# Turned rows kept in memory, and a pair's full-precision work in one stretch, in a kernel of two MoE layers around a state-space layer

## The chip, the cores and the metric

The kernel runs on one core of a Trainium2 chip. The metric is the device time of one execution in microseconds (us), taken as the median of several runs. Another execution was recorded by the hardware profiler; its rows are the source of all durations below. Engines are called PE (TensorE), ACT (ScalarE), DVE (VectorE), POOL (GpSimd) and SP (SyncE, which issues most DMAs here).

## The reference, cut to what matters

4096 tokens (2 x 2048) of 512 values pass through three parts: a feed-forward (FFN) layer, a state-space layer (Mamba-2), and the same FFN layer again with the same weights; each is added to its input. The change lies in the FFN:

```python
h = layernorm(x)                                  # eps 1e-5, no weights
logits = h @ router_w.T                           # 64 experts
topk_idx = top_k(logits + bias, 4); topk_w = softmax scores of these, summing to 1
out  = sum over experts e: scatter(topk_w * (silu(h_e @ gate_w[e].T) * (h_e @ up_w[e].T)) @ down_w[e].T)
out += (silu(h @ sh_gate.T) * (h @ sh_up.T)) @ sh_down.T   # shared expert, 1024 wide
x = x + 0.5 * out
```

Each expert has 64 slots (CAP) for tokens and an inner width of 128.

## The kernel before, in words

`ffn` builds one FFN; it is called twice, with the tags a and b (`prior` is set for b), and `mamba` stands between. All three are pieces of one program on each engine, and the order on each engine is written out by hand: an engine runs its instructions strictly in order, and semaphores join them.

**Blocks and units.** The shared expert goes through 16 blocks of 256 tokens (NS, BS). A block has 4 units (UN), each of which computes 256 of the 1024 inner columns: `gate_or_up` for the gate (24 matmuls of 256 columns), the same for up, and `down` of the unit before (12 matmuls of 512 columns). These run in a faster fp32 format (fp32r) with every operand split into a high and a low part, `three` matmuls for one product. Between the three parts stand positions g = 3u, 3u+1, 3u+2, where other work is put in.

**Turning the rows for the shared expert.** The matmuls need the normalised tokens turned, with the 512 features on the partitions: `hts_hi[b % 2]` and `hts_lo[b % 2]`. For each block ACT's `normed` makes `hs` from the rows `xs` (two passes, L580 and L585), PE's `turn_s` (L724) turns it in two halves of 4 transposes, into the PSUM bank `p_ts`, ACT's `turned_s` (L590) copies the high part and DVE's (L1009) the rest. For block b+1 this is done in units 1 to 3 of block b.

**Routing.** In blocks 0 to 7 the router works on 512 tokens (r = b, that is blocks 2r and 2r+1): DVE's `norm_apply` writes the normalised rows `hr`, PE's `turn_r` turns slice k (of 4) into `p_x0` (L766), ACT's and DVE's `turned_r` copy it into `htr_hi[k % 2]` and `htr_lo[k % 2]` (L609, L951), and `logits_turned` multiplies (L778). Slices 0 and 1 come in unit 0, slices 2 and 3 in unit 1; on ACT slice 2 comes ahead of `product_hi` of unit 1. So the same rows are turned twice, once here and once in `turn_s`. POOL sends the rows to their experts' slots in memory (L459), and clears (L468, L499).

**Pairs.** The 64 experts are taken as 32 pairs, from unit 39 on, two pairs in each unit. For pair q: SP loads rows and weights (`load_pair`, three buffers), PE turns the rows (`turn_rows`, L803), multiplies (`expert_gate_up`, L814, into columns 0 to 255 of `p_x1`), turns the product (`turn_prod`, L821, into further columns of `p_x1`) and does `expert_down` (L829); all that is in full fp32. `begins`, `turns_rows` and `turns_product` say at which position what is done; the turned product stands in the middle of a gate or behind up. ACT copies the result into one of 5 buffers `y` (L636), and POOL adds it to the output in memory (`add_pair`, L479), each addition waiting for the one before; blocks 10 to 13 are added in the same chain (`add_block`, L475). At the end of FFN b POOL's `merge` (L485) adds the second half of the output to the first in memory.

**SP.** One list for each block: the load of the next 512 tokens `xr` (L420), the store of the finished block before (L423), then, over the positions, pairs and the rows `xs` of the block after next (`load_xs`, L350).

Of the kernel before, what the change touches and what calls it, by code (L numbers as in the profile page):

```python
# [13 lines left out]
P = 128  # L14
# [168 lines left out]
def ffn(nc, tag, c, sems, src, acc, xg, shw, routw, routb, ew, first_token, clear_slots, merge_all, prior=None):  # L183
# [13 lines left out]
    with ExitStack() as ctx:  # L197
# [70 lines left out]
        xs_loaded, x_stored = [sem(f"xs_loaded{u}") for u in range(XB)], sem("x_stored")  # L268
        hs_mid, hs_ready, ts_full = sem("hs_mid"), sem("hs_ready"), sem("ts_full")
# [27 lines left out]
        turned_in = lambda b, half: p_gate if b == 0 and half == 1 else p_ts  # L297
# [12 lines left out]
        def turns_rows(g):  # L310

            u, p = divmod(g, 3)
            q = 2 * (u - PAIR_UNIT) + p
            return q if p > 0 and 0 <= q < PAIRS else None

        def turns_product(g):


            u, p = divmod(g, 3)
            q = 2 * (u - PAIR_UNIT) + (0 if p == 1 else -1)  # L320
            return q if p < 2 and 0 <= q < PAIRS else None
# [20 lines left out]
        def sync(sp):  # L342
# [9 lines left out]
            def load_pair(q):  # L352
# [12 lines left out]
                sp.dma_start(w[u][:], ew[q]).then_inc(w_loaded[u], 16)  # L365

# [34 lines left out]
            def program():  # L401
# [42 lines left out]
        def gpsimd(pool):  # L444
# [46 lines left out]
            def program():  # L491
# [43 lines left out]
                pool.wait_ge(hs_mid, NS * TS)  # L535
# [22 lines left out]
        def scalar(act):  # L558
# [10 lines left out]
            def normed(b):  # L569
                rows_of = xs[:, b % XB, :, :]  # L570
                if b == 0 and not prior:
                    rows_of = xr
                else:
                    act.wait_ge(xs_loaded[b % XB], 16 * (b // XB + 1))
                act.wait_ge(mean_ready, norms(b * TS))
                act.wait_ge(rstd_ready, norms(b * TS))
                wait(act, ts_full, 2 * b)
                for j in range(TS):
                    at = b * TS + j
                    a.activation(hs[:, j, :], rows_of[:, j, :], ACT.Identity,  # L580
                                 bias=neg_mean[:, at:at + 1]).then_inc(hs_mid, 1)
                for j in range(TS):
                    at = b * TS + j
                    act.wait_ge(hs_mid, at + 1)
                    a.activation(hs[:, j, :], hs[:, j, :], ACT.Identity,  # L585
                                 scale=rstd[:, at:at + 1]).then_inc(hs_ready, 1)

            def turned_s(b, half):
                act.wait_ge(ts_full, 2 * b + half + 1)
                a.activation(hts_hi[b % 2][:, 2 * half:2 * half + 2, :], turned_in(b, half)[:, :, :], ACT.Copy).then_inc(hts_hi_ready, 1)  # L590
# [47 lines left out]
            def experts_at(g):  # L638
                q = begins(g)
                if q is not None and q < PAIRS:  # L640
                    expert_silu(q)
                if q:
                    expert_out(q - 1)
                q = turns_rows(g)
                if q is not None:
                    rows_out(q)

            def early(step):
                if step == 0:

                    act.wait_ge(prior.x_stored[2], 16 * len(range(2, NM, XM)))
                    normed(0)
                if step == 1:
                    split(0)
                    turned_s(0, 0)
                    turned_s(0, 1)
# [4 lines left out]
            def program():  # L661
                if not prior:
                    split(0)
                    normed(0)
                    turned_s(0, 0)
                    turned_s(0, 1)
# [5 lines left out]
                for b in range(NS):  # L672
                    for u in range(UN):
                        i, g = b * UN + u, b * POS + 3 * u
                        routes, more = b < NR, b + 1 < NS
# [9 lines left out]
                        if more and u == 2:  # L685
                            turned_s(b + 1, 0)
                        if more and u == 3:
                            turned_s(b + 1, 1)
# [9 lines left out]
                        if more and u == 1:  # L698
                            normed(b + 1)
# [9 lines left out]
        def tensor(pe):  # L709
# [7 lines left out]
            def turn_s(b, half):  # L717
                pe.wait_ge(hs_ready, (b + 1) * TS)
                if b > 0:
                    pe.wait_ge(hts_ready, 2 * b + half)  # L720
                for kk in range(2):
                    k = 2 * half + kk
                    for j in range(TS):
                        mm = t.matmul(turned_in(b, half)[:, kk, j * P:(j + 1) * P], hs[:, j, k * P:(k + 1) * P], c.ident[:],  # L724
# [3 lines left out]
            def gate_or_up(i, g, out, full, free):  # L728
                b, u = divmod(i, UN)
                if g == 0 and u == 0:  # L730
                    pe.wait_ge(hts_ready, 2 * b + 2)
# [75 lines left out]
            def expert_gate_up(q):  # L807
# [3 lines left out]
                wait(pe, pt_ready, q)  # L811
# [20 lines left out]
            def experts_at(g):  # L832
                q = begins(g)
                if q is not None and q < PAIRS:
# [1356 lines left out]
```

## Time and profile before

| what | value |
|---|---|
| median of 3 runs | 2375.12 us (2374.7 to 2375.79) |
| the profiled execution | 2374.74 us, of which the recorded span is 2373.0 us |
| PE busy | 2328.0 us (98%), 16700 matmuls |
| DVE, ACT, POOL busy | 59%, 40%, 29% |
| FFN a, state space, FFN b | about 0 to 720, 720 to 1640, 1620 to 2373 us |
| granted TensorE clock | 0.994 over the span |
| DMA | mean 123 GB/s; 254 to 289 GB/s in the stretches with pairs |

The span is what the profiler recorded; the execution's own time is 1.7 us more. The busy time of PE sums durations that overlap, so the share says that PE hardly rests, not what one matmul costs; for that the starts in the timeline are read. FFN b begins while the state-space part ends, since the parts overlap by some instructions.

### The profile page before, as it was taken

To read this page: it belongs to the slowest core of one execution; us is meant where nothing else is said; L and a number is where in the kernel's file an instruction comes from. 1 tells how busy PE (TensorE), PEld (TensorE's weight loads), DVE (VectorE), ACT (ScalarE), POOL (GpSimd) and SP (SyncE) were. 2 spreads that over 40 slices of the span, in tenths; PEclk is the share of its full clock that TensorE was granted. 3 is DMA by queue.
4 is the path that set the end of the run, shared out by engine and by line. 5 is a ranking of instruction groups with operands and counts; after the bars stand their busy time and mean duration, and the time that the engine had idled before them with its cause. 6 is when DMAs were issued, how large, how long until landed. Compare 5 with 4: busy or idle time off the path is not lost.

```text
span 2373.0 us, 41894 instructions
## 1 busy us (share of the span) xinstructions
PE 2328.0 (98%) x16700; PEld 2059.6 (87%) x16700; DVE 1393.6 (59%) x3240; ACT 950.3 (40%) x1650; POOL 680.9 (29%) x526
## 2 busy tenths in 40 slices
PE   6999999999999999999999999999999999999997
PEld 6999999777788899998998898998999999877787
DVE  6777762223228777777777777778777763222221
ACT  5333322333327455554545555455433232323331
POOL 1244443111220323232322222321144444112121
PEclk9999999999999999999999999999999999999999
DMA  8644213899844111111111111104263411799958
GB/s 265 205 144 153 86 64 126 261 279 282 253 93 133 36 36 28 28 28 28 27 28 27 28 27 28 28 19 161 74 222 109 141 65 37 254 289 287 276 106 176
DMA packets 102785, 292.81 MB, mean 123 GB/s; under 512 B 22530, under 2 KB 22786, under 8 KB 91904
## 3 DMA queue, kind: packets, MB, share of 16 engines
q1 hardware_dynamic: 55248, 198.87, 23.3%
q0 software_dynamic: 47344, 91.27, 17.3%
q8 instruction: 133, 2.18, 0.4%
q14 instruction: 60, 0.49, 0.1%
HBM read 197.28 MB, written 151.80 MB: 147 GB/s over the span
## 4 chain that ended last, share of the span: by engine, by line
PE 96%; DVE 2%; ACT 1%; issue 1%; DMA 0%; DVEq 0%; POOL 0%; SPq 0%; ACTq 0%
PE m_p_ab L1614 5%; PE m_p_ab L1615 5%; PE m_p_ab L1616 5%; PE m_p_x L1616 3%; PE m_p_x L1615 3%; PE m_p_x L1614 3%; PE p_up_b L713 3%; PE p_up_a L713 3%; PE p_gate_a L713 3%; PE p_up_b L715 3%; PE p_up_b L714 3%; PE p_gate_b L713 3%; PE p_gate_a L715 3%; PE p_gate_a L714 3%; PE p_up_a L715 3%; PE p_up_a L714 3%
## 5 line engine op out<-in xcount | busy, mean ns | idle before, releaser
L1927 DVE SCALAR_TENSOR_TENSOR m_xt<-m_ssm,m_convw,m_xt 128x256 f32<-128x256 f32 x384 | 219.1, 584 | 58.1 <-ACT m_ssm L1483 48.9
L459 POOL DMA_INDIRECT slot_rows<-a_hr,a_slot_now x128 | 130.4, 1019 | 152.1 <-PE p_gate_a L715 96.5
L459 POOL DMA_INDIRECT slot_rows<-b_hr,b_slot_now x128 | 130.3, 1018 | 151.8 <-PE p_gate_b L715 96.5
L1614 PE MATMUL m_p_ab<-m_ht_hi,m_wi_b_hi 128*128 128x256 f32 x576 | 163.6, 284 | 3.3 <-ACT m_gate L1455 3.3
L1615 PE MATMUL m_p_ab<-m_ht_lo,m_wi_b_hi 128*128 128x256 f32 x576 | 161.7, 281 | 0.0
L1616 PE MATMUL m_p_ab<-m_ht_hi,m_wi_b_lo 128*128 128x256 f32 x576 | 161.7, 281 | 0.0
L713 PE MATMUL p_gate_a<-a_hts_hi,a_w_hi 128*128 128x256 f32 x512 | 149.4, 292 | 1.7 <-DVE a_hts_lo L1009 1.4
L713 PE MATMUL p_up_a<-a_hts_hi,a_w_hi 128*128 128x256 f32 x512 | 147.9, 289 | 0.0
L713 PE MATMUL p_gate_b<-b_hts_hi,b_w_hi 128*128 128x256 f32 x512 | 147.4, 288 | 0.3
L713 PE MATMUL p_up_b<-b_hts_hi,b_w_hi 128*128 128x256 f32 x512 | 147.7, 288 | 0.0
L1389 POOL TENSOR_TENSOR m_state_dec<-m_state,m_etot 128x1024 f32<-128x1024 f32 x31 | 74.0, 2387 | 255.4 <-ACT m_etot L1499 255.4
L715 PE MATMUL p_gate_a<-a_hts_hi,a_w_lo 128*128 128x256 f32 x512 | 146.3, 286 | 0.0
L714 PE MATMUL p_gate_a<-a_hts_lo,a_w_hi 128*128 128x256 f32 x512 | 146.2, 285 | 0.0
L715 PE MATMUL p_up_a<-a_hts_hi,a_w_lo 128*128 128x256 f32 x512 | 144.8, 283 | 0.0
L715 PE MATMUL p_up_b<-b_hts_hi,b_w_lo 128*128 128x256 f32 x512 | 144.7, 283 | 0.0
L714 PE MATMUL p_up_a<-a_hts_lo,a_w_hi 128*128 128x256 f32 x512 | 144.6, 282 | 0.0
L715 PE MATMUL p_gate_b<-b_hts_hi,b_w_lo 128*128 128x256 f32 x512 | 144.4, 282 | 0.0
L714 PE MATMUL p_up_b<-b_hts_lo,b_w_hi 128*128 128x256 f32 x512 | 144.4, 282 | 0.0
L714 PE MATMUL p_gate_b<-b_hts_lo,b_w_hi 128*128 128x256 f32 x512 | 144.3, 282 | 0.0
L1015 DVE TENSOR_TENSOR b_prod<-b_silu,p_up_b 128x512 f32<-128x512 f32 x64 | 44.0, 687 | 165.0 <-PE p_up_b L715 164.5
L1015 DVE TENSOR_TENSOR a_prod<-a_silu,p_up_a 128x512 f32<-128x512 f32 x64 | 44.0, 687 | 149.0 <-PE p_up_a L715 148.1
L1481 ACT ACTIVATE m_xt<-m_p_ab,m_convb,m_convw 128x256 f32<-128x256 f32 x128 | 72.2, 564 | 143.4 <-PE m_p_ab L1616 143.4
(374 smaller groups left out, 7518.8 us busy)
## 6 DMA issues: line engine op xcount, KB each, us to landing
a_ew<-in_ew SPq DMA_DIRECT2D x32, 1536.0 KB, 7.6
b_ew<-in_ew SPq DMA_DIRECT2D x32, 1536.0 KB, 7.3
after_ffn<-a_zeros POOLq DMA_DIRECT2D x6, 2048.0 KB, 9.2
out<-b_zeros POOLq DMA_DIRECT2D x6, 2048.0 KB, 9.2
slot_rows<-a_zeros POOLq DMA_DIRECT2D x1, 8336.0 KB, 40.0
a_rows<-slot_rows SPq DMA_DIRECT2D x32, 260.5 KB, 8.0
b_rows<-slot_rows SPq DMA_DIRECT2D x32, 260.5 KB, 8.1
a_xs<-in_x SPq DMA_DIRECT2D x16, 512.0 KB, 4.2
```

Source lines behind the costliest of these rows:

```text
L459: g_.indirect_dma_start(out=xg, out_offset=bass.IndirectOffsetOnAxis(ap=slot_now[r % HR][:, at:at + 1], axis=0), in_=hr[r % HR][:, j, :], ...
L713: t.matmul(out, l_hi, r_hi_, start=first, stop=False)
L714: t.matmul(out, l_hi, r_lo_, start=False, stop=False)
L715: return t.matmul(out, l_lo, r_hi_, start=False, stop=last)
L1015: v.tensor_tensor(prod[:, i % 2, :, :], silu[:, i % 2, :, :], p_up[:, :, :], ALU.mult).then_inc(prod_ready, 1)
L1389: g.tensor_tensor(state_dec[:], state[:], etot[:, j, :].unsqueeze(2).to_broadcast([P, NH, HP]), ALU.mult).then_inc(state_dec_ready, 1)
L1481: a.activation(xt[:, m, :], ab_of(J_SSM[m])[:, 0:BM], ACT.Identity, bias=convb[:, m:m + 1], scale=convw[:, m, HALO:CONV]).then_inc(tap_rea ...
L1614: t.matmul(out, l_hi, r_hi_, start=first, stop=False)
L1615: t.matmul(out, l_hi, r_lo_, start=False, stop=False)
L1616: return t.matmul(out, l_lo, r_hi_, start=False, stop=last)
L1927: ins_ = v.scalar_tensor_tensor(xt[:, m, :], ssm[:, m, i:i + BM], convw[:, m, i:i + 1], xt[:, m, :], ALU.mult, ALU.add)
```

## The change

1. The high and low turned parts of the router's pass are stored to a new tensor in memory, `turned`, [16 blocks, 128, 2, 1024], by `store_turned`: for each slice k two stores of 256 KB with runs of 1 KB. `load_turned` brings them back for blocks 1 to 15, two loads of 512 KB with 4 KB per partition. `normed`, `turn_s` and `turned_s` remain for block 0 alone.
2. ACT's copy of slice k into `htr_hi` now also waits until the stores of slice k-2 have landed (`turned_stored`), and the first gate of blocks 1 to 15 waits for `hts_loaded`.
3. For each pair PE now does at one position: the turned product of the pair before, gate/up of this pair, the rows of the next, down of the pair before. `turns_rows` and `turns_product` are gone; the turned product goes to the bank `p_ts`, which is free there now.
4. `finish` waits for `xs_loaded` itself, and the two waits elsewhere that counted `hs_mid` and `ts_full` are rewritten.

The diff, cut to its core:

```diff
+        turned_stored, hts_loaded = [sem(f"turned_stored{u}") for u in range(2)], sem("hts_loaded")
...
+        FIRST_ROWS = 3 * PAIR_UNIT - 1
...
+            def store_turned(r, k):
+
+                for i, (part, ready) in enumerate(((htr_hi, htr_hi_ready), (htr_lo, htr_ready))):
+                    sp.wait_ge(ready, r * KD + k + 1)
+                    sp.dma_start(turned[2 * r:2 * r + 2, :, i, k * BS:(k + 1) * BS].rearrange("b p t -> p b t"),
+                                 part[:, k % 2, :].bitcast(F32).rearrange("p (b t) -> p b t", b=2)).then_inc(turned_stored[k % 2], 16)
+
+            def load_turned(b):
+                for v in range(2):
+                    sp.wait_ge(turned_stored[v], 32 * (KD // 2) * (b // 2 + 1))
+                if b >= 2:
+                    sp.wait_ge(up_full, (b - 1) * UN)
+                for i, part in enumerate((hts_hi, hts_lo)):
+                    sp.dma_start(part[b % 2][:, :, :].bitcast(F32).rearrange("p k t -> p (k t)"),
+                                 turned[b, :, i, :]).then_inc(hts_loaded, 16)
...
+                    if b < NR:
+                        store_turned(b, 0)
                     if 1 <= b <= NR + 1:
                         sp.wait_ge(acc_ready, b * TS)
                         sp.dma_start(acc_s[b - 1], xs[:, (b - 1) % XB, :, :]).then_inc(x_stored, 16)
+                    if b < NR:
+                        for k in range(1, KD):
+                            store_turned(b, k)
+                    if b + 1 < NS:
+                        load_turned(b + 1)
...
-                pool.wait_ge(hs_mid, NS * TS)
+                pool.wait_ge(xs_loaded[(NS - 1) % XB], 16 * ((NS - 1) // XB + 1))
...
                 if f >= 2:
                     act.wait_ge(lt_done, f - 1)
+                    act.wait_ge(turned_stored[k % 2], 32 * (f // 2))
                 a.activation(htr_hi[:, k % 2, :], p_x0[:], ACT.Copy).then_inc(htr_hi_ready, 1)
...
+                if g == 0 and u == 0 and b > 0:
+                    pe.wait_ge(hts_loaded, 32 * b)
...
-                    if g == 0 and m == 1 and turns_product(3 * i) is not None:
-                        turn_prod(turns_product(3 * i))
...
-                t.matmul(p_x1[:, 2 * F:2 * F + P], eprod[:, q % 2, :], c.ident[:],
+                t.matmul(p_ts[:, 0, 0:P], eprod[:, q % 2, :], c.ident[:],
...
             def experts_at(g):
                 q = begins(g)
+                if g == FIRST_ROWS:
+                    turn_rows(0)
+                if q:
+                    turn_prod(q - 1)
                 if q is not None and q < PAIRS:
                     expert_gate_up(q)
+                if q is not None and q + 1 < PAIRS:
+                    turn_rows(q + 1)
                 if q:
                     expert_down(q - 1)
-                q = turns_product(g)
-                if q is not None and g % 3:
-                    turn_prod(q)
-                q = turns_rows(g)
-                if q is not None:
-                    turn_rows(q)
...
-                        if more and u == 3:
-                            turn_s(b + 1, 1)
```

How the instructions move, at two places. First PE, a unit with pairs in FFN a. Before, behind up stand the turned product (of `a_eprod`) and rows of a pair, and behind `down` the gate/up (`a_ew`, `a_xt`), down (`a_pt`) and rows of others (two pieces):

```order
L715 MATMUL p_up_a<-a_hts_hi_55,a_w_lo 128x256
L821 MATMUL p_x_a<-ident,a_eprod 128x128
L803 MATMUL p_x_a<-ident,a_rows_96 128x128 x4
L713 MATMUL p_out_a<-a_w_hi,a_act_hi 128x512
L714 MATMUL p_out_a<-a_w_lo,a_act_hi 128x512
```

```order
L715 MATMUL p_out_a<-a_w_hi,a_act_lo 128x512
L814 MATMUL p_x_a<-a_ew_99,a_xt 64x256 x8
L829 MATMUL p_x_a<-a_ew_98,a_pt 64x512 x2
L803 MATMUL p_x_a<-ident,a_rows_94 128x128 x4
L713 MATMUL p_gate_a<-a_hts_hi_55,a_w_hi 128x256
L714 MATMUL p_gate_a<-a_hts_lo_56,a_w_hi 128x256
```

With the change the four kinds stand together, here behind `down`; nothing stands behind up, and the line numbers are the changed file's:

```order
L724 MATMUL p_out_a<-a_w_hi,a_act_lo 128x512
L827 MATMUL p_ts_a<-ident,a_eprod 128x128
L820 MATMUL p_x_a<-a_ew_99,a_xt 64x256 x8
L810 MATMUL p_x_a<-ident,a_rows_94 128x128 x4
L835 MATMUL p_x_a<-a_ew_98,a_pt 64x512 x2
L722 MATMUL p_gate_a<-a_hts_hi_55,a_w_hi 128x256
L723 MATMUL p_gate_a<-a_hts_lo_56,a_w_hi 128x256
```

The turned product now goes ahead of a gate/up, and rows stand between gate/up and down.

Second, SP at the start of FFN a (`a_hr_71`, `a_xs` and `a_hr_72` are also the staging places of the weights). Before, behind the last piece of weights:

```order
L350 DMA a_xs<-in_x 128x2x512
L420 DMA a_xr<-in_x 128x4x512
L350 DMA a_xs<-in_x 128x2x512
L420 DMA a_xr<-in_x 128x4x512
L423 DMA after_ffn<-a_xs 128x2x512
L350 DMA a_xs<-in_x 128x2x512
```

With the change, from the load of `xr` for routing block 1 on to the load of `xs` for block 2:

```order
L428 DMA a_xr<-in_x 128x4x512
L363 DMA turned_rows<-a_htr_hi 128x2x256
L363 DMA turned_rows<-a_htr_lo 128x2x256
L363 DMA turned_rows<-a_htr_hi 128x2x256
L363 DMA turned_rows<-a_htr_lo 128x2x256
L363 DMA turned_rows<-a_htr_hi 128x2x256
L363 DMA turned_rows<-a_htr_lo 128x2x256
L363 DMA turned_rows<-a_htr_hi 128x2x256
L363 DMA turned_rows<-a_htr_lo 128x2x256
L372 DMA a_hts_hi_55<-turned_rows 128x1024
L372 DMA a_hts_lo_56<-turned_rows 128x1024
L342 DMA a_xs<-in_x 128x2x512
```

All eight stores and the two loads of block 1 stand ahead of the load of `xs`, and each store waits for its copy.

## Rows read from the trace of the kernel before

**Rows 1.** The page: chain of waits by engine, and the SP queue's bytes and share.
```profile
q1 hardware_dynamic: 55248, 198.87, 23.3%
...
PE 96%; DVE 2%; ACT 1%; issue 1%; DMA 0%; DVEq 0%; POOL 0%; SPq 0%; ACTq 0%
```

**Rows 2.** Groups of PE by line and form: xcount, busy us, mean ns, idle before.
```profile
L724 PE MATMUL p_ts_a<-ident,a_hs 128*128 128x128 f32 x124 | 19.0, 277 | 11.7 <-ACT a_hs L585 11.7
```

**Rows 3.** PE's timeline around one turning group: start us, us, engine, line, what.
```profile
290.78 0.60 PE L724 MATMUL p_ts_a<-ident,a_hs 128*128 128x128 f32 x4
291.13 0.48 PE L713 MATMUL p_out_a<-a_w_hi,a_act_hi 128*128 128x512 f32 x1
291.45 0.39 PE L714 MATMUL p_out_a<-a_w_lo,a_act_hi 128*128 128x512 f32 x1
291.68 0.39 PE L715 MATMUL p_out_a<-a_w_hi,a_act_lo 128*128 128x512 f32 x1
```

**Rows 4.** PE's timeline, turned rows of pairs in FFN a and what follows.
```profile
507.54 0.60 PE L803 MATMUL p_x_a<-ident,a_rows 128*128 128x128 f32 x4
507.89 0.48 PE L713 MATMUL p_out_a<-a_w_hi,a_act_hi 128*128 128x512 f32 x1
...
513.61 0.66 PE L803 MATMUL p_x_a<-ident,a_rows 128*128 128x128 f32 x4
514.02 0.37 PE L713 MATMUL p_gate_a<-a_hts_hi,a_w_hi 128*128 128x256 f32 x1
```

**Rows 5.** Block 0 of FFN b: timelines of SP, ACT, PE; median us to landing.
```profile
1656.78 0.51 SPq L350 DMA_DIRECT2D b_xs<-after_mamba  x1
...
b_xs<-after_mamba SPq DMA_DIRECT2D x1, 512.0 KB, 7.9
...
1657.86 0.60 ACT L609 ACTIVATE b_htr_hi<-p_x_b 128x512 fp32r<-128x512 f32 x1 [0.20 <-PE p_x_b L766]
...
1661.00 0.60 PE L766 MATMUL p_x_b<-ident,b_hr 128*128 128x128 f32 x4
```

**Rows 6.** Block 0 of FFN a: timelines of SP and ACT; us to landing.
```profile
32.06 0.51 SPq L350 DMA_DIRECT2D a_xs<-in_x  x1
...
a_xs<-in_x SPq DMA_DIRECT2D x1, 512.0 KB, 6.9
...
36.24 0.60 ACT L609 ACTIVATE a_htr_hi<-p_x_a 128x512 fp32r<-128x512 f32 x1
```

**Rows 7.** Block 2 of FFN a: SP's store of a block, its landing, and PE.
```profile
113.52 0.37 SPq L423 DMA_DIRECT2D after_ffn<-a_xs  x1
...
after_ffn<-a_xs SPq DMA_DIRECT2D x1, 512.0 KB, 5.8
...
119.57 0.60 PE L766 MATMUL p_x_a<-ident,a_hr 128*128 128x128 f32 x4
```

**Rows 8.** POOL's timeline in FFN b, additions of pairs (in brackets: idle before, releaser).
```profile
2211.66 1.63 POOL L479 DMA_INDIRECT out<-b_y,b_row_no  x1 [11.88 <-DMA out<-b_xs]
...
2261.70 1.56 POOL L479 DMA_INDIRECT out<-b_y,b_row_no  x1 [4.38 <-ACT b_y L636]
...
2276.47 1.63 POOL L479 DMA_INDIRECT out<-b_y,b_row_no  x1 [5.69 <-DMA out<-b_xs]
...
2305.87 1.55 POOL L479 DMA_INDIRECT out<-b_y,b_row_no  x1 [4.38 <-issue]
```

**Rows 9.** Windows (busy us of PE, PEld, DVE, ACT, POOL; PEclk, DMA share, GB/s); end.
```profile
2100.00:2200.00 100.00, 100.00 (x713) 75.52 (x712) 30.22 (x124) 30.10 (x60) 20.07 (x13) 1.00 0.90 273
2290.00:2300.00 10.00, 10.00 (x74) 9.46 (x73) 2.67 (x4) 1.83 (x3) 1.78 (x3) 1.00 0.42 52
2325.00:2360.00 35.00, 35.00 (x236) 32.03 (x235) 6.81 (x10) 4.91 (x8) 3.54 (x4) 1.00 1.04 212
...
q0 software_dynamic: 460, 2.43, 103.1%
...
2359.67 0.39 PE L715 MATMUL p_out_b<-b_w_hi,b_act_lo 128*128 128x512 f32 x1
```

More of the change, by code:

```diff
@@ L295, in ffn @@
                  hr[2][:, :, :].rearrange("p j d -> p (j d)")[:, 0:PIECE]]
-        turned_in = lambda b, half: p_gate if b == 0 and half == 1 else p_ts
+        turned_in = p_ts, p_gate
         norms = lambda at: at // TS + 1 if at < TR else at // TR + 2
@@ L567, in split, with normed, turned_s @@
                 a.activation(w_hi[:, i * PIECE:(i + 1) * PIECE], stage[slot_of[o]], ACT.Copy).then_inc(w_hi_done, 1)
-            def normed(b):
-                rows_of = xs[:, b % XB, :, :]
-                if b == 0 and not prior:
-                    rows_of = xr
[L573 to L577, printed above, removed]
+            def normed():
+                rows_of = xs[:, 0, :, :]
+                if prior:
+                    act.wait_ge(xs_loaded[0], 16)
+                else:
+                    rows_of = xr
+                act.wait_ge(mean_ready, 1)
+                act.wait_ge(rstd_ready, 1)
                 for j in range(TS):
-                    at = b * TS + j
                     a.activation(hs[:, j, :], rows_of[:, j, :], ACT.Identity,
-                                 bias=neg_mean[:, at:at + 1]).then_inc(hs_mid, 1)
+                                 bias=neg_mean[:, j:j + 1]).then_inc(hs_mid, 1)
                 for j in range(TS):
-                    at = b * TS + j
-                    act.wait_ge(hs_mid, at + 1)
+                    act.wait_ge(hs_mid, j + 1)
                     a.activation(hs[:, j, :], hs[:, j, :], ACT.Identity,
[L586 to L590, printed above, removed]
+                                 scale=rstd[:, j:j + 1]).then_inc(hs_ready, 1)
+            def turned_s(half):
+                act.wait_ge(ts_full, half + 1)
+                a.activation(hts_hi[0][:, 2 * half:2 * half + 2, :], turned_in[half][:, :, :], ACT.Copy).then_inc(hts_hi_ready, 1)
             def gate_silu(i):
@@ L674, in program @@
                         i, g = b * UN + u, b * POS + 3 * u
-                        routes, more = b < NR, b + 1 < NS
+                        routes = b < NR
                         gate_silu(i)
@@ L715, in three, with turn_s @@
                 return t.matmul(out, l_lo, r_hi_, start=False, stop=last)
[L717 to L720, printed above, removed]
+            def turn_s(half):
+                pe.wait_ge(hs_ready, TS)
                 for kk in range(2):
@@ L723, in turn_s @@
                     for j in range(TS):
-                        mm = t.matmul(turned_in(b, half)[:, kk, j * P:(j + 1) * P], hs[:, j, k * P:(k + 1) * P], c.ident[:],
+                        mm = t.matmul(turned_in[half][:, kk, j * P:(j + 1) * P], hs[:, j, k * P:(k + 1) * P], c.ident[:],
                                       is_transpose=True, start=True, stop=True)
@@ L862, in program @@
                         i, g = b * UN + u, b * POS + 3 * u
-                        routes, more = b < NR, b + 1 < NS
+                        routes = b < NR
                         if i > 0 or not prior:
@@ L880, in program @@
                             logits_turned(b, 2)
-                        if more and u == 2:
-                            turn_s(b + 1, 0)
                         if routes and u == 3:
@@ L1024, in finish @@
                 dve.wait_ge(down_done, (b + 1) * UN)
-                if b == 0 and not prior:
-                    dve.wait_ge(xs_loaded[0], 16)
+                dve.wait_ge(xs_loaded[b % XB], 16 * (b // XB + 1))
                 if b == NS - 1:
@@ L1098, in program @@
                         i, g = b * UN + u, b * POS + 3 * u
[L1099 removed]
+                        routes = b < NR
                         if routes and u == 0 and b > 0:
@@ L2104, in build @@
         with Phase(nc) as s:
-            first = ffn(nc, "a", c, s, ins["x"], after_ffn, xg, *weights, 0, True, False)
+            first = ffn(nc, "a", c, s, ins["x"], after_ffn, xg, turned, *weights, 0, True, False)
             state_space = first.follow = mamba(nc, c, s, after_ffn, after_mamba, ins, first)
```

83 lines of the change are left out of this document (32 added, 51 removed).

## The prediction

> **What bounds the kernel now.** I read the chain of waits first, because it says which engine's time is the kernel's time: 96% of it is TensorE (PE) [rows 1]. PE is therefore worth a second look at every edit, and DVE and ACT only where somebody waits for them. Then I read PE's groups by line for what is removed [rows 2], PE's timeline for what such a piece takes of the engine, which is less than its duration [rows 3, 4], the block that starts each FFN for the new waits [rows 5, 6], a routing block in a busy stretch [rows 7], and last the queue of the GpSimd (POOL) and the DMA load at the end [rows 8, 9]. That last look matters most: from 2325 to 2360 us the DMA engines are busy all the time [rows 9], with the software queue's merges alone, and PE's last matmul starts at 2359.67. The end is thus held by two things at once, and only one of them gets shorter by PE's savings.
>
> The sum is made against the profiled execution, 2374.7 us (span 2373.0); the median of the runs is 2375.1. I count 0.2%, 4.8 us, as what a measurement can tell from no change.
>
> **Removed: the turning of the shared expert's rows.** Blocks 1 to 15 of each FFN lose two groups of four turnings each, 60 groups and 240 matmuls in all. One turning lasts 277 ns [rows 2], but they overlap: from the group's start at 290.78 to the next matmul at 291.13 are 0.35 us, and the matmul behind takes 0.32 us to its successor where the next takes 0.23 [rows 3]. So a group costs 0.35 + 0.09 = 0.44 us of PE. 30 groups x 0.44 = 13.2 us in each FFN. The Trainium skill (TensorE: Matmul & The Clock Gate, Part 4: PE-mode transpose) gives about 275 ns for one 128x128 transpose in a kernel. The trace agrees for the duration, and by that figure as a cost the 240 would be worth 66 us; the spacing in the timeline decides against it. ACT loses four scalings and two copies for each block, DVE two subtractions; neither is on the chain there, so I count nothing.
>
> **Moved: the pairs' work.** Per unit of two expert pairs PE had four excursions into full precision (product in the middle of a gate, pair work after gate, product and rows after up, pair work after down) and now has two. Leaving one costs about 0.09 us, as above, so two fewer give 0.2 us. Against it, rows turned directly behind full-precision work take 0.41 us instead of 0.35 [rows 4], once more per unit. How a turned product sits ahead of a pair's first matmul no row shows: between 0 and 0.1 us each. That leaves 0 to 0.3 us per unit, 0 to 5 us for 16 units; I take 2. The product's copy on DVE is now hidden by the gate/up and rows matmuls of the same stretch, where DVE is idle but for the two adds that close a block.
>
> **Added: the store, and who waits for it.** For each routing block SP issues 8 stores of 256 KB, and for each block from 1 on two loads of 512 KB. The copy of the k-th slice (ACT) now waits until the store of slice k-2 has landed. Behind that copy stand DVE's low half, PE's next turning and, on ACT, a weight split and the hi half of the product. In steady blocks the store of slice 0 goes out behind the 1 MB load of the next rows, so it lands about where the store of 512 KB lands now: in the busiest block issued at 113.52 and 5.8 us under way, so at 119.3, just when PE wants to turn slice 3, at 119.57 [rows 7]; the copy takes 0.6 us [rows 5] and the low half about as much again. I take 1.5 us for FFN a and 0.5 for b, between nothing and 1.5 per block.
>
> Block 0 is worse. In FFN b SP comes to its loop only after a 1 MB piece; today the load issued at 1656.78 takes 7.9 us, to 1664.7 [rows 5]. The store of slice 0 takes its place. The copy of slice 2, at 1657.86 today, moves to about 1664.5, the low half is ready at 1666, and PE, which today turns slice 3 at 1661.00, waits 4.5 us; the last slice adds about 1, and the clock may fall after the idle time, so 6 us. In FFN a the same place is taken by a load issued at 32.06 that lands 6.9 us later, at 39.0, against a copy at 36.24 [rows 6]: 2 us. A store is twice as many and half as large packets as that load, so both could be longer. The loads of turned rows for block 1 are needed only about two units after the last store, and later ones have two units of slack; I count nothing. If that cover goes, PE waits at the first gate of a block.
>
> FFN a: -13.2 - 2 + 2 + 1.5 = -11.7 us.
>
> **The end of FFN b.** From the second pair on, POOL's additions form a chain in which each waits for the one before [rows 8]. It runs far behind PE: the last addition starts at 2305.87, while PE's last pair is in unit 55 of 64. It is followed by a block, by reads and by the merges that fill the engines to the end. What PE gains after the chain has begun it cannot pass on. Before that point FFN b has 20 of its 30 groups: -8.8 us, + 6 + 0.5 of waits, so -2.3 us. During the chain four blocks load 1 MB each. At 23.3% of the span for 198.87 MB [rows 1] one such load takes 2.9 us of all engines, in 62 us a share of 0.05. An addition takes 50.04/7 = 7.15 us at a share of 0.90 and 29.4/5 = 5.9 at 0.42 [rows 8, 9], 2.6 us per unit of share, so 0.13 x 30 = 4 us later. The bounds are 0, and 12 us if each load simply stands ahead of the chain. In FFN a the same lag first shows in ACT's wait for a free y buffer; from there to PE there is about one pair's distance, 7 us, which I take as enough. With that cover gone PE would wait for `y_ready`.
>
> Sum: -11.7 - 2.3 + 4 = -10.0 us, so 2364.7, against 2374.7. PE itself would end 20 us earlier and then wait for nobody.
>
> **Rivals.**
> (1) PE sets the end after all: the merges start as much earlier as PE does. Then FFN b gives -13.2 - 2 + 6.5 = -8.7 and the time is 2374.7 - 20.4 = 2354.3. The full DMA engines speak against it [rows 9]. Chance 0.09.
> (2) The stores land fast: each store is half of the transfers in [rows 5 to 7], and packets of two queues may share better than I think. Then the waits of 2 + 1.5 + 6 + 0.5 go, and the time is 2354.7. Chance 0.11. The Trainium skill (DMA: Bandwidth & Descriptors, Anatomy of one DMA) gives 2.0 us plus bytes/436 GB/s, an estimate of 2.6 us for 256 KB, and this case would be its result; the rows of loaded queues (5.8 to 7.9 us) are above it.
> (3) A turning costs its duration: 60 groups at 0.60 us. FFN a then gains 18 instead of 13.2 and b 12 instead of 8.8 before its chain: 2356.7. Chance 0.02.
> (4) The chain of additions is hit harder: 12 us in b and some 4 us of PE waiting for y in a. 2364.7 + 8 + 4 = 2376.7. The share of 0.90 speaks for it. Chance 0.17.
> (5) Slower: the stores' small packets share the engines with the software queue's large ones, and the copy of slice 2 or 3 is late in every routing block, not in block 0 alone. At 2 us for 13 of them, less the 2 counted, it is +24: 2388.7. It turns into a loss from about 0.9 us per block. The block of [rows 7] is at the edge; the others' traffic is lighter. Chance 0.15.
>
> **How the numbers follow.** My case has 0.46, its own range 2356 to 2373. With rivals 1 to 3, faster by over 0.2% (under 2370.4) comes to 0.67, a few of my own case lying above; within 0.2% is rival 4 and that rest, 0.18; slower is rival 5, 0.15. The range takes in rival 1 and rival 4: 2353 to 2378.
>
> **What would show it.** PE's rows on the turning of hs fall from 248 matmuls to 16. The copy L609 (its line will move) shows waits for a DMA in block 0: some 6 us in b, 3 in a, and under 1 elsewhere; PE shows one idle time of 4 to 5 us at slice 3 of b. FFN b's first addition comes 13 to 15 us earlier, the last one some 10, and the DMA engines are full until the end while PE stops 8 us or more ahead of them. I am wrong if PE's end still sets the span, if the copy waits in steady blocks, or if the first gate of a block waits for its load.

## The result, and the profile after

The changed kernel takes 2403.95 us (median of 4 runs, 2403.28 to 2410.25) against 2375.36 beside it (2374.7 to 2375.79): a ratio of 1.0111, 95% interval 1.0088 to 1.0135. It is 28.6 us slower; the predicted gain was 10. The profiled spans differ by the same amount, 2401.6 against 2373.0, so the traces can carry the explanation. At the first silu of FFN b 18.3 us of the loss have come up, the other 10.3 come in FFN b.

First the page of the changed kernel: TensorE's busy time, the SP queue, the chain of waits by engine, and two groups of PE (busy us, mean ns).

```profile
PE 2326.4 (97%) x16460; PEld 2033.5 (85%) x16460; DVE 1360.8 (57%) x3180; ACT 854.9 (36%) x1470; POOL 677.4 (28%) x526
q1 hardware_dynamic: 98704, 263.90, 31.3%
PE 92%; DMA 4%; DVE 2%; ACT 1%; issue 1%; SPq 0%; POOL 0%; DVEq 0%; ACTq 0%
...
L731 PE MATMUL p_ts_a<-ident,a_hs 128*128 128x128 f32 x4 | 1.1, 427 | 11.5 <-ACT a_hs L598 11.5
L835 PE MATMUL p_x_a<-a_ew,a_pt 128*64 128x512 f32 x128 | 34.5, 617 | 0.4 <-DVE a_pt L1054 0.4
```

The turnings are gone (4 of 124 are left in p_ts_a, [rows 2]), 240 matmuls in all, but PE's busy time is only 1.6 us below the 2328.0 of before. The SP queue moves 65 MB more than in [rows 1], in 43456 more packets, and DMA has 4% of a chain that had none. Next, who waits (us in total, times, longest), for PE and for ACT.

```profile
PE p_x_a L773 <- DVE a_htr_lo L953: 10.0, 4, 5.4
PE p_x_b L773 <- DVE b_htr_lo L953: 9.6, 5, 6.6
PE p_gate_a L722 <- DMA a_hts_lo<-turned_rows: 8.5, 1, 8.5
PE p_x_a L785 <- DVE a_htr_lo L953: 5.7, 1, 5.7
...
ACT a_htr_hi L623 <- DMA turned_rows<-a_htr_lo: 19.0, 5, 8.7
ACT b_htr_hi L623 <- DMA turned_rows<-b_htr_lo: 13.9, 4, 8.6
```

These are large waits but few: ACT's copy of a slice waits 9 times in 64. PE's first two sums hold one wait each that is not new: 5.4 us before the turning at 28.89, where the kernel before waits 4.9, and 2.0 at 1671.65, the same as before. To find where the time goes I laid the two traces side by side, by the start of ACT's 64 silus in each FFN; a step in the distance is a place of gain or loss.

| place | change against before |
|---|---|
| FFN a, block 0 from second to third unit | +12.4 us |
| FFN a, first unit of block 1 | +10.4 |
| FFN b, block 0 from second to third unit | +8.5 |
| each removed group of turnings | -0.43 |
| blocks 2 and 3 of both FFNs (a: 1.4; b: 0.7 and 0.5) | +2.6 in all |
| each unit that works on two pairs | +0.65 |
| end: from PE's last matmul to the end of the span | +4.3 |

With 60 groups (-25.8) and 15 such units in each FFN (+19.5) these come to 31.9. The first unit of block 0 in FFN a gives 1.7 back and the stretch between the FFNs 1.0; 0.6 are left over.

The first place, in SP's timeline of FFN a's block 0 (start, us, line, what):

```profile
31.46 0.40 SPq L428 DMA_DIRECT2D a_xr<-in_x  x1
31.90 0.51 SPq L363 DMA_DIRECT2D turned_rows<-a_htr_hi  x1
...
41.51 1.00 SPq L363 DMA_DIRECT2D turned_rows<-a_htr_lo  x1
52.03 0.36 SPq L363 DMA_DIRECT2D turned_rows<-a_htr_hi  x1
52.76 0.36 SPq L363 DMA_DIRECT2D turned_rows<-a_htr_lo  x1
70.68 0.33 SPq L372 DMA_DIRECT2D a_hts_hi<-turned_rows  x1
```

and ACT's and PE's timelines (in brackets the idle time before, and what ended it), with the windows of 10 us (busy us of PE, PEld, DVE, ACT, POOL; then granted clock, DMA share, GB/s):

```profile
40.16 0.60 ACT L623 ACTIVATE a_htr_hi<-p_x_a 128x512 fp32r<-128x512 f32 x1 [5.28 <-DMA turned_rows<-a_htr_lo]
51.41 0.60 ACT L623 ACTIVATE a_htr_hi<-p_x_a 128x512 fp32r<-128x512 f32 x1 [8.68 <-DMA turned_rows<-a_htr_lo]
...
81.90 0.58 PE L722 MATMUL p_gate_a<-a_hts_hi,a_w_hi 128*128 128x256 f32 x1 [8.54 <-DMA a_hts_lo<-turned_rows]
...
50.00:60.00 10.00, 7.21 (x47) 7.02 (x48) 5.60 (x18) 1.79 (x3) 1.03 (x1) 0.71 1.03 282
70.00:80.00 10.00, 3.36 (x27) 2.47 (x25) 6.91 (x14) 0.64 (x1) 0.00 (x0) 0.82 1.06 234
80.00:90.00 10.00, 8.10 (x50) 8.10 (x51) 0.00 (x0) 0.60 (x1) 0.00 (x0) 0.67 0.40 155
```

Three things stand in these rows. The DMA engines are full (1.03, 1.06): POOL's clearing of the slots, 8336 KB, runs from about 34 to 80 us. Of the 256 KB stores the one of 41.51 takes 19.4 us to land and that of 52.76 takes 17.9; the load for block 1 can't be issued before, and lands 10.8 us later. And behind the idle times TensorE's granted clock is below full (0.71, 0.67), which makes each wait dearer than its own length. Behind the wait of 8.5 us the gate's matmuls first follow each other after 0.21 us instead of 0.12, and the delay is 10.4 us. In block 0 PE idles 1.2, 2.2 and 5.7 us, 9.1 in all, and the delay is 12.4.

### The profile page after: what moved, and what is told of

It is laid out like the page before. It is cut to its first block, busy times and chain, and to the rows that moved or that the text cites. A ratio compares the mean times of both kernels' runs of the same rounds, so it can differ in the third digit from the quotient of the medians.

```text
span 2401.6 us, 41242 instructions
## 1 busy us (share of the span) xinstructions
PE 2326.4 (97%) x16460; PEld 2033.5 (85%) x16460; DVE 1360.8 (57%) x3180; ACT 854.9 (36%) x1470; POOL 677.4 (28%) x526
## 4 chain that ended last, share of the span: by engine, by line
PE 92%; DMA 4%; DVE 2%; ACT 1%; issue 1%; SPq 0%; POOL 0%; DVEq 0%; ACTq 0%
PE m_p_ab L1610 5%; PE m_p_ab L1611 4%; PE m_p_ab L1612 4%; PE m_p_x L1612 3%; PE m_p_x L1611 3%; PE m_p_x L1610 3%; PE p_up_b L722 3%; PE p_gate_b L722 3%; PE p_gate_a L722 3%; PE p_x_a L820 3%; PE p_x_b L820 3%; PE p_up_a L722 2%; PE p_out_b L722 2%; PE p_up_b L724 2%; PE p_up_b L723 2%; PE p_out_b L724 2%
```

## The experiments

Each ran beside the kernel before. In these runs the kernel before spread over 2372 to 2392 us, so each time is read by its ratio, and the mechanism by the distance of the silus to those of the kernel before in the first trace. e11 is the changed kernel again; its distance was 15.9 us at block 1 of FFN a, where the first trace has 21.2, so the sizes of the waits in blocks 0 and 1 vary by some 5 us.

**e1: the pairs in their old order, memory kept.** The functions `experts_at` of PE, ACT and DVE, `turns_rows` and `turns_product` as before, and

```
-                t.matmul(p_ts[:, 0, 0:P], eprod[:, q % 2, :], c.ident[:],
+                t.matmul(p_x1[:, 2 * F:2 * F + P], eprod[:, q % 2, :], c.ident[:],
```

> Turned rows still go through memory; only the pairs' instructions stand again where they stood before the change (turned product back in p_x1, in the middle of the next gate matrix). Theory 'alternation' (the one stretch costs 0.65 us a unit over 32 units because TensorE changes four times between turning and full-precision multiplying): about 21 us come back, 2403.9 -> 2383 us, and the pairs' units take what they took before (6.91 us above a plain unit). Rival 'traffic' (the pairs slow down because the turned rows' loads share the DMA engines with the pairs' weights): the time stays within 4 us of 2404. Rival 'both in halves': 2390 to 2396.

Measured: 2408.36, ratio 1.0132 (1.0098 to 1.0166). Nothing came back, although the +0.65 did go: from block 10 to 12 the distance to before falls from 10.6 to 9.0 us, only the removed turnings' share. Then it jumps by 10.5 us in block 12 of FFN a and by 3.9 in FFN b, and from PE's last matmul to the end of the span are 23.9 us (17.7 in the changed kernel, 13.3 before). The waits from 550 to 640 us:

```profile
POOL after_ffn L502 <- ACT a_y L658: 66.6, 9, 10.3
ACT a_y L658 <- DMA after_ffn<-a_y,a_row_no: 39.1, 8, 12.4
...
PE p_x_a L830 <- DVE a_pt L1064: 8.7, 2, 6.6
```

ACT's copy into one of the five y buffers waits for an addition, up to 12.4 us; behind it on ACT stands the rows' copy, and TensorE runs dry. The first line is the same wait seen from POOL, as I read it: each addition also waits for the one before, and the one issued at 609.99 lets ACT's copy start at 621.14 and the next addition at 621.90. SyncE too is held in e1: its wait for the addition of a block (`load_xs`) is 43.3 us in FFN a's pairs, 18.8 before. So neither theory held: the order was worth 0.65 us a unit, and TensorE could not use it.

**e2: the two turnings side by side.** In the stretch turned product, turned rows, gate and up, down:

```
+                if q is not None and q + 1 < PAIRS:
+                    turn_rows(q + 1)
                 if q is not None and q < PAIRS:
                     expert_gate_up(q)
-                if q is not None and q + 1 < PAIRS:
-                    turn_rows(q + 1)
```

> The one stretch in the order turned product, turned rows, gate and up, down (so that the two turnings stand together and TensorE changes twice, not four times); ScalarE copies the rows out ahead of the silu. Theory 'alternation': the stretch falls by two changes, 0.1 to 0.6 us a unit, time 2385 to 2399 us. Rival 'bank' (it is the wait for the turned product in the freed bank, copied by VectorE, that costs): that wait only comes nearer or stays, time 2403 +- 2 or up to 6 us more, because gate and up now also wait for ScalarE's copy of the rows.

Measured: 2409.68, ratio 1.0142 (1.0106 to 1.0178). The time missed the expectation: 9.7 us are lost over block 12 of FFN a and 7.9 over that of FFN b. In FFN a the stall comes by another way than in e1. SyncE waits 14.7 us for the addition of a block, ahead of the loads for the pairs; it issues the rows' load at 607.70, and PE waits 7.0 us for these rows at 611.42. But the stretch shows the price. PE's timeline of the changed kernel and of e2:

```profile
543.99 0.27 PE L827 MATMUL p_ts_a<-ident,a_eprod 128*128 128x128 f32 x1
544.19 1.95 PE L820 MATMUL p_x_a<-a_ew,a_xt 128*64 128x256 f32 x16
546.07 0.66 PE L810 MATMUL p_x_a<-ident,a_rows 128*128 128x128 f32 x4
546.66 1.08 PE L835 MATMUL p_x_a<-a_ew,a_pt 128*64 128x512 f32 x4
547.66 0.38 PE L722 MATMUL p_gate_a<-a_hts_hi,a_w_hi 128*128 128x256 f32 x1
```

```profile
541.13 0.27 PE L827 MATMUL p_ts_a<-ident,a_eprod 128*128 128x128 f32 x1
541.24 0.60 PE L810 MATMUL p_x_a<-ident,a_rows 128*128 128x128 f32 x4
541.77 1.95 PE L820 MATMUL p_x_a<-a_ew,a_xt 128*64 128x256 f32 x16
543.55 1.03 PE L835 MATMUL p_x_a<-a_ew,a_pt 128*64 128x512 f32 x4
544.50 0.39 PE L722 MATMUL p_up_a<-a_hts_hi,a_w_hi 128*128 128x256 f32 x1
```

The same 25 matmuls take 547.66 - 543.99 = 3.67 us in one order and 544.50 - 541.13 = 3.37 in the other. The difference of 0.30 lies at four places: the product is followed after 0.20 instead of 0.11 us, gate and up after 1.88 instead of 1.78, the rows after 0.59 instead of 0.53, down after 1.00 instead of 0.95.

Is that the price of every place where a turning meets full-precision work? The kernel before has such places too, behind down:

```profile
526.44 0.40 PE L715 MATMUL p_out_a<-a_w_hi,a_act_lo 128*128 128x512 f32 x1
526.77 1.95 PE L814 MATMUL p_x_a<-a_ew,a_xt 128*64 128x256 f32 x16
528.55 1.03 PE L829 MATMUL p_x_a<-a_ew,a_pt 128*64 128x512 f32 x4
529.51 0.66 PE L803 MATMUL p_x_a<-ident,a_rows 128*128 128x128 f32 x4
529.92 0.36 PE L713 MATMUL p_gate_a<-a_hts_hi,a_w_hi 128*128 128x256 f32 x1
```

For each kind of stretch I took what it adds to PE's time: from the start of the matmul ahead of it to the start of the second matmul behind it, less the two steps of undisturbed split work (0.12 us for 256 columns, 0.23 for 512). The medians ("rows" are four turnings as well):

| stretch | kernel | adds, us | places |
|---|---|---|---|
| product | before | 0.11 | 32 |
| four turnings of hs | before | 0.45 | 4 |
| product, rows | before | 0.55 | 24 |
| gate/up, down | before | 2.93 | 21 |
| four turnings of hs, gate/up, down | before | 3.37 | 5 |
| gate/up, down, rows | before | 3.32 | 23 |
| product, gate/up, rows, down | changed | 3.78 | 49 |
| product, rows, gate/up, down | e2 | 3.48 | 49 |

A turning ahead of gate/up costs no more than the two apart (3.37 for 0.45 + 2.93; 3.48 for 0.55 + 2.93), and rows behind down cost some 0.05 less than apart. Only the rows between gate/up and down are dear: they cut the full-precision work in two, and that is the 0.30. Where it begins, the piece ahead takes some 0.09 us more, be it split work (0.33 instead of 0.23 at 526.44) or a turning (0.20 instead of 0.11). A unit of the kernel before adds 0.11 + 2.93 + 0.55 + 3.32 = 6.91 us, one of the changed kernel 2 x 3.78 = 7.56, one of e2 2 x 3.48 = 6.96. These are the +0.65 and the +0.05 of the silus.

**e3: the clearing of the slots later.**

```
-                    pool.wait_ge(w_lo_done, PIECES)
+                    inv_std(1)
+                    pool.wait_ge(hts_loaded, 32)
```

> FFN a's clearing of the slots (8.3 MB on POOL's queue, 45.6 us) starts only when block 1's turned rows have been loaded, so that it shares no DMA engine with the first stores. Theory 'shared engines': the stores of 256 KB land in 2.5 to 4 us instead of 7 to 19, the waits of 5.7 + 5.4 us and half a block's in FFN a's block 0 and 1 go, and about 20 us of the time with them: 2382 to 2388 us; FFN b's +8.5 stays. Rival 'small packets' (the stores' 1 KB pieces are slow by themselves): landings stay over 6 us and the time over 2396 us. Risk: the first rows are sent to the slots later, which POOL alone waits for.

Measured: 2407.14, ratio 1.0108 (1.0068 to 1.0147): no gain, yet it tells most. The distance to before is only 4.1 us at block 1's start (15.9 in e11) and grows by 14.0 us between the second and third unit of block 1, beside the clearing, now issued at 53.03. ACT's copy in block 1:

```profile
53.03 1.88 POOL L515 DMA_DIRECT2D slot_rows<-a_zeros  x1 [2.95 <-DMA a_hts_lo<-turned_rows]
...
93.74 0.60 ACT L625 ACTIVATE a_htr_hi<-p_x_a 128x512 fp32r<-128x512 f32 x1 [13.15 <-DMA turned_rows<-a_htr_lo]
```

The wait follows the clearing, so the clearing is its cause. And where the clearing is gone, the last slice of block 0 is copied at 44.07 without a wait, at 51.41 in the changed kernel. A wait of 6.6 us stays in block 0: there the store stands behind the 1 MB load of the next rows, as in FFN b. Block 0 of FFN a still loses 6.2 us by it. No landing time of a store stands in e3's trace, so what the small packets cost by themselves stays open; in the later blocks of e4, with the same packets, the waits are at most 2.2 us.

**e4: blocks 0 and 1 turned as before.** `normed`, `turned_s` and `turn_s` take the block again for b = 1, and

```
-                    if b < NR:
+                    if 1 <= b < NR:
                         store_turned(b, 0)
-                    if b + 1 < NS:
+                    if 1 <= b and b + 1 < NS:
                         load_turned(b + 1)
```

> Only blocks 0 and 1 are normed and turned by ScalarE and TensorE as before the change; the routing's turned rows of blocks 0 and 1 are not stored, from block 2 on everything goes through memory, the pairs stay in one stretch. Theory: the waits of blocks 0 and 1 go in both FFNs (about 23 us in a, 8.5 us in b) less 4 turnings that return (4 x 0.44), so 2373 to 2378 us. Rival 'stores late in every routing block' (the wait only moves to the next first use, block 2): no more than 8 us are gained, 2396 us or more.

Measured: 2381.23, ratio 0.9998 (0.9981 to 1.0015). The profiled span is 20.3 us below e11's (2375.8 against 2396.1), the largest single step. At block 2 the distance is -0.7 us in FFN a and -0.3 in b, against +15.0 and +20.6 in e11 (in b with what FFN a had lost); and the stores of later blocks make no such wait:

```profile
ACT a_htr_hi L625 <- DMA turned_rows<-a_htr_lo: 5.0, 3, 2.2
ACT b_htr_hi L625 <- DMA turned_rows<-b_htr_lo: 2.9, 2, 2.1
```

The rival of stores that are late in every routing block is out.

**e5: e1 without the loads of blocks 10 to 15** (`load_turned(b + 1)` only for b up to NR; blocks 10 to 15 are multiplied with the turned rows of 8 and 9).

> As e1 (pairs' instructions where they stood before the change), and the turned rows of blocks 10 to 15 are not loaded: TensorE multiplies those of blocks 8 and 9 again in their place, so the output of those blocks is another. Theory 'chain' (in e1 the saved 0.65 us a unit came back as stalls, because 1 MB more per block slows POOL's serial additions, SyncE waits for the block's addition ahead of the pairs' loads, and TensorE runs out of rows): without the loads SyncE's wait for the block's addition falls from 43 to about 19 us in each FFN, no stall of 10 us is left, and the time is 2380 to 2388 us against e1's 2408. Rival 'order' (the pairs' old order stalls behind memory in the changed kernel whatever the traffic): still over 2400 us.

Measured: 2381.67, ratio 1.0027 (1.0001 to 1.0054). No jump is left in either FFN (the distance goes from 9.1 at block 10 to 4.0 at block 15, and in b from 4.9 to -0.2), and SyncE's wait for a block's addition is 19.2 and 21.1 us:

```profile
SPq L350 <- DMA after_ffn<-a_xs: 19.2, 2, 14.3
```

As the theory of the chain had it: 1 MB more per block beside additions that are nearly back to back is enough to make TensorE wait. How often such a stall comes, one trace each does not show; this one is the fastest of e5's ten executions, and four of the others took 2389 to 2401 us.

**e6: e4 with the input rows loaded a block later**, so that SyncE waits for no addition there.

```
-                        if g == b * POS + 6 and b + 2 < NS:
-                            load_xs(b + 2)
+                        if g == b * POS + 6 and 1 <= b and b + 1 < NS:
+                            load_xs(b + 1)
```

> As e4, and each block's input rows for the sum are loaded one block later (block b's in block b - 1, not b - 2: with the turned rows from memory nothing reads them earlier), so that SyncE no longer waits for a block's addition ahead of the pairs' loads. TensorE did not stall in e4's pairs, so by the theory nothing is gained there: within 3 us of e4 (2378 to 2384 on that chip, ratio 0.998 to 1.002).

Measured: 2382.58, ratio 1.0007 (0.9991 to 1.0023), as expected of the time; but its profiled execution, the slowest of ten with a span of 2389.1, lost 4 us over block 13 of FFN a, where ACT waited 36.4 us for additions in all. The stalls are not bound to the pairs' old order.

**e7 and e8: e4 with the pairs' old order, with and without e6's edit.** The diffs are those of e1, e4 and e6.

> Three edits together: blocks 0 and 1 turned as before (e4), pairs' instructions where they stood before the change (e1), and input rows loaded one block later, so that SyncE isn't held by the addition chain. Theory: the stalls of e1 (10 us in FFN a, 4 in b) go because SyncE isn't held, TensorE's work ends 10 us earlier in each FFN than in e4; FFN a gives that to Mamba in full, FFN b ends with the chain of additions: 2364 to 2372 us, ratio to before 0.994 to 0.998. Rival 'the chain itself is full' (additions take more time than TensorE needs for a unit, and ScalarE's copy waits for the fifth addition back whatever SyncE does): TensorE waits on the chain instead, 2374 us or more.

> As e7 without the later loads: e4 and e1 together. By the theory SyncE is held as in e1 (35 to 43 us per FFN) and TensorE stalls 4 to 10 us in each FFN: 2372 to 2382 us. If it is as fast as e7, SyncE's hold was not what carried the stalls of e1.

Measured: e7 2391.94, ratio 1.0059 (1.0036 to 1.0083); e8 2388.19, ratio 1.0032 (1.0012 to 1.0053). Both are worse than e4, though PE is 5 us ahead of it by block 12. e7's theory fell and its rival stands: with SyncE no longer held by an addition, ACT still waits for additions, FFN a loses 7.0 us in block 13 and FFN b 8.2 in block 12 (-4.87 to +3.30 from its second unit on). e8, expected at 2372 to 2382, is no slower than e7, and its trace loses 8.7 us over block 12 of FFN a.

```profile
ACT b_y L660 <- DMA out<-b_y,b_row_no: 64.6, 16, 12.2
```

SyncE's hold is thus not needed for the stall. The additions leave little room: in e1, e7 and e8 what speeds TensorE up beside them is taken back, in lumps.

**e9 and e12: memory only for blocks 2 to 9.** Blocks 0, 1 and 10 to 15 are normed and turned as before, the pairs stand in the old order:

```
+        BY_TURN = [b for b in range(NS) if not 2 <= b <= 9]
+                if g == 0 and u == 0 and b not in BY_TURN:
+                    pe.wait_ge(hts_loaded, 32 * (b - 1))
```

> Turned rows through memory only for blocks 2 to 9, ahead of the pairs; blocks 0, 1 and 10 to 15 are normed and turned by ScalarE and TensorE as before the change, and the pairs' instructions stand where they stood. Theory: no wait in blocks 0 and 1, no added traffic beside the pairs, 16 turnings of 0.44 us gone from each FFN: both chains of additions start 7 us earlier; 7 us in FFN a and 5 to 7 us in FFN b, ratio 0.994 to 0.995 to before (about 12 to 14 us). Rival 'the additions hold the time anyway' (their chain doesn't start earlier, or stalls as in e1): ratio 0.998 to 1.003.

Measured: 2379.18, ratio 0.9993 (0.9973 to 1.0013). The trace explains it: -5.9 us at the end of block 9 in FFN a (7 expected), then +0.97 in each of the blocks 10 to 13; FFN b also loses 4.3 us in block 13. In my version DVE's second subtraction stood behind its waits for the pair. e12 puts both of its subtractions back (against e9):

```
+                        if b + 1 in BY_TURN and u == 3:
+                            turned_s(b + 1, 1)
                         experts_at(g + 2)
-                        if b + 1 in BY_TURN and u == 3:
-                            turned_s(b + 1, 1)
```

> As e9 with VectorE's two subtractions for the next block's turned rows back exactly where they stood before the change (ahead of its waits for the pair; in e9 the second stood behind them, and each of the blocks 10 to 15 lost 0.97 us at its start). Theory: the 0.97 us of those blocks go, TensorE's last matmul comes 6 us earlier in each FFN than in e9, each FFN is 7 us shorter than before; 10 to 14 us in all, ratio 0.994 to 0.996. Rival 'additions and merges hold the end': FFN a gives 7 us, FFN b nothing, ratio 0.997; or stalls in the pairs eat both: 0.998 to 1.002.

Measured: 2371.41 (2361.82 to 2379.92) beside 2379.76, **ratio 0.9971 (0.9953 to 0.9989)**: it beats both kernels. FFN a is 6.25 us ahead of before and keeps it; FFN b goes from -5.9 to -10.3 and loses 5.4 in block 13. ACT waits 23.0 us in all for additions in FFN b. That is the first rival's case, with its ratio of 0.997: FFN a gives its part, FFN b nothing in the end.

**e10: the changed kernel without the loads of blocks 10 to 15.**

> The changed kernel whole, one stretch included, but the turned rows of blocks 10 to 15 are not loaded (those of blocks 8 and 9 stand in for them, so that the output of those blocks is another). If the traffic costs time only by way of the additions: TensorE's pair units keep their +0.65 us (they did not wait), and the end of FFN b, which waits for the additions, comes 3 to 5 us nearer to TensorE's last matmul: 3 to 6 us less than e11. Rival 'the traffic itself slows the pair units': +0.65 falls to under 0.3 and about 15 us go.

Measured: 2402.03, ratio 1.0101 (1.0066 to 1.0135), against e11's 1.0123 (1.0084 to 1.0161): within the noise of each other, so the 3 to 6 us expected do not show. The +0.65 per unit is unchanged (11.32, 11.97 in the second and third unit of block 10), so the rival of traffic that slows the units is out. From the start of the last matmul to the end of the span are 16.0 us, against 17.0 in e11 and 13.3 before: of the 4 us lost there 1 goes with the traffic, little more than the 0.7 by which the two traces of the changed kernel differ there (17.7 and 17.0).

**e11: the changed kernel again.**

> The changed kernel without any edit, on the chip of the other runs of this study, so that e1 to e10 have it beside them: 2404 +- 5 us, ratio 1.009 to 1.014. Rival 'the stalls of e1 are that chip's': the changed kernel also shows a stall of 4 us or more in its pairs here.

Measured: 2404.25, ratio 1.0123 (1.0084 to 1.0161), and no stall in its pairs: ACT waits 2.2 and 2.4 us for additions. Slowed by its own order, TensorE doesn't outrun them here.

**e13: the order alone.** The kernel before with the one stretch; the turned product goes to p_ts between two turnings, which needs two more waits on PE.

```
+                pe.wait_ge(hts_ready, halves[0])
-                t.matmul(p_x1[:, 2 * F:2 * F + P], eprod[:, q % 2, :], c.ident[:],
+                t.matmul(p_ts[:, 0, 0:P], eprod[:, q % 2, :], c.ident[:],
```

> The kernel before with the pairs' order alone: nothing through memory, all blocks normed and turned as before; the pair's work in one stretch, its turned product in the bank p_ts between the turnings of the next block's rows. Theory 'alternation' (0.65 us a unit, 32 units, whatever the memory traffic): 15 to 22 us slower than before, ratio 1.006 to 1.010. Rival 'the order costs only with the traffic': ratio 0.998 to 1.003.

Measured: 2395.82, ratio 1.0076 (1.0052 to 1.0101), with no turned row in memory. The distance grows by 9.9 us in FFN a and 10.1 in FFN b, 0.65 in the units without other moves, and no wait answers to it; PE's only one in FFN a's pairs is:

```profile
PE p_x_a L822 <- DVE a_pt L1046: 0.4, 1, 0.4
```

The order costs by itself what the first table gives it. Its stretches add 3.78 us each, as in the changed kernel.

## Why the prediction was wrong

FFN a was forecast at -11.7 us and came out at +18.3, FFN b at +1.7 and came out at +10.3. Two steps failed: the price of the pairs' order, and the first two blocks of FFN a.

- **Turnings, -13.2 us per FFN: right.** Each group gave 0.43 us, for 0.44 worked out from the spacing in [rows 3]. The 277 ns of duration [rows 2] would have been too much, so rival 3 is out.
- **The pairs' order, -2 in FFN a and nothing in b: the step that failed by its sign.** It measured +9.9 and +10.1 (e13). I counted excursions out of the split form as the unit of cost and took 0.2 us a unit for two fewer. That saving is not there: product and rows together with gate/up and down add 3.48 us, 0.55 and 2.93 apart. What costs is how often full precision begins, twice a unit before and four times now, since the rows of the next pair cut gate/up from down: 0.30 us for each cut, two in a unit. I had priced the cut with 0.06 (0.41 against 0.35 us, [rows 4]) and the product ahead of gate/up with 0 to 0.1; gate and up ahead of the rows (+0.10) and down behind them (+0.05) I had at nothing. The last 0.05 is what rows behind down had saved in the kernel before.
- **Block 0 of FFN a, +2: mis-sized, 22.8 measured over blocks 0 and 1** (some 16.5 in e11). I took the landing of a 512 KB load at 32.06 [rows 6] for that of the stores. The stores stand where the clearing has begun, and those issued from 35.36 on take 14 to 19 us. And "the loads of turned rows for block 1 are needed only about two units after the last store", counted as nothing, failed: with stores that late the first gate waited 8.5 us, 10.4 with the clock (1.4 us of waiting in e11). The mechanism, ACT's copy waiting for the store two slices back, was the one I named; e3 shows that the clearing causes all but some 6 us of it, e4 that the whole term goes when blocks 0 and 1 are turned as before.
- **Block 0 of FFN b, +6: right in kind, 8.5 measured.** The copy of slice 2 comes at 1684.87 after 8.6 us of waiting for the store of 1675.93, PE idles 6.6 us, and the clock is at 0.70 from 1680 to 1690.
- **Steady blocks, 1.5 and 0.5: near**, 1.4 and 1.2. Rival 5, the loss in every routing block, had the right sign and the wrong place: the loss is in two blocks.
- **The additions, +4 at the end: the size is right (4.3), the reason only in part.** PE was not ahead of the chain, as I had it, but 24 us late, so that the chain had time to wait for PE (first addition at 2063.57 instead of 2043.59). The last merges went out at 2348.30, 27 us later than in the kernel before. The DMA engines are full until 2390, and the last stores, issued at 2385.09, land 7.6 us later. 1.6 us of it are turnings saved behind the last pair: there the distance of the silus falls from 25.9 to 24.3, and only PE ends earlier by that. e10 gives the added loads 1 us; what the rest is stays open. That PE can't pass on what it gains beside the chain fits the runs: in e1 and e7, where PE's last matmul is 4 and 21 us less behind than in the changed kernel, the end comes 23.9 and 25.0 us after its last matmul.
- "7 us of distance, which I take as enough" for FFN a's y buffers held in the changed kernel, but only because its order slowed PE. In e1 that cover goes and 10.5 us are lost at once. That is the answer to rival 4: its wait is real, and in the changed kernel hidden behind the order's own cost.
- On the landing of a store: the Trainium skill (DMA: Bandwidth & Descriptors, Anatomy of one DMA) led to 2.6 us for 256 KB in rival 2. That section is on the path of the GpSimd queue, while these stores are on SyncE's, and it prices one transfer by itself. The rows here are 7.2 to 19.4 us in block 0, behind and beside megabytes, so rival 2 is out; the measurement decides.

## What to carry to other kernels

Count how often full-precision work begins, and put no turning between two pieces of it: each such cut cost 0.30 us here. The same turnings ahead of it, behind it or among work in the split form cost what they cost anywhere (0.11 us each), and putting them into one stretch with it saved nothing. Where memory replaces an engine, place the transfers by who shares the DMA engines in that very block, and leave the first blocks, beside clears and weight loads, on the engine. And where a serial chain of additions keeps pace with the engine that sets the time, work taken off that engine beside the chain is no gain; take it off ahead of the chain (e12).

## What the runs showed of the hardware

A 256 KB store beside the 8336 KB clearing landed after 14 to 19 us, one behind a 1 MB load after 7 to 9. TensorE's granted clock was 0.71 and 0.67 of full speed in the 10 us windows with idle times of 5.7 and 8.5 us, partly at 1.2 GHz therefore. Four turnings between two pieces of full-precision work made the stretch 0.30 us longer than ahead of both, with no wait in the trace; ahead of them a turning cost 0.11 us, as elsewhere. And TensorE lost 4 to 10 us in one lump in the pairs of several kernels (e1, e2, e6, e7, e8, e9, e12), each time beside waits for an addition.
